# A chunked scan: the state contribution of a row on four column quarters, and placed last in TensorE's turn

## The reference

```
dA_cs  = cumsum(dt * A)                                       # within a chunk
att    = (C B^T) * exp(dA_cs_i - dA_cs_j) * dt_j, causal      # 128 x 128 per head
y      = att @ x  +  exp(dA_cs) * (C @ state)  +  D * x
state  = state * exp(dA_cs[last])  +  B^T @ (exp(dA_cs[last] - dA_cs) * dt * x)
out    = (layernorm(y) * norm_w + norm_b) * z @ out_proj_w^T
```

## Time and profile before

| | us |
|---|---|
| median of 3 runs | 2703.73 |
| lowest and highest | 2697.77, 2711.97 |
| the profiled execution, its own time | 2695.24 |
| its span, first to last instruction | 2693.3 |
| busy PE, PEld, DVE, ACT, POOL | 2309.8, 1650.3, 1685.5, 1305.3, 1184.2 |

### The profile page before, as it was taken

How to read it: one execution, slowest core, us unless ns; L and a number is a source line. 1 busy time by engine, 2 the same in 40 slices (tenths; PEclk the granted TensorE clock), 3 DMA queues, 4 the chain that set the end, 5 groups by cost and what they waited for, 6 DMA issues and landing times. The chain is left out here.

```text
span 2693.3 us, 61840 instructions
## 1 busy us (share of the span) xinstructions
PE 2309.8 (86%) x21973; PEld 1650.3 (61%) x22100; DVE 1685.5 (63%) x3119; ACT 1305.3 (48%) x2719; POOL 1184.2 (44%) x1381
## 2 busy tenths in 40 slices
PE   0798888998758189999999999999987988879888
PEld 0565536796657057777777777777766655356553
DVE  5345475675535278777777777777773454734547
ACT  0345440281057156666666666666643454334543
POOL 0332250000000168788888888888853222532225
PEclk9999998999979589999999999999998999989999
DMA  8613495415523222222222222222215034950349
GB/s 197 188 52 71 109 312 143 90 50 165 131 75 120 102 51 52 53 54 51 51 53 54 51 51 53 54 51 51 54 50 168 20 72 111 310 176 26 70 107 315
DMA packets 287144, 270.22 MB, mean 100 GB/s; under 512 B 157102, under 2 KB 220366, under 8 KB 280730
## 3 DMA queue, kind: packets, MB, share of 16 engines
q1 hardware_dynamic: 276218, 254.04, 33.6%
q0 software_dynamic: 9280, 6.44, 2.0%
q10 hardware_dynamic: 1496, 7.63, 0.8%
HBM read 163.34 MB, written 81.46 MB: 91 GB/s over the span
## 5 line engine op out<-in xcount | busy, mean ns | idle before, releaser
L1608 ACT ACTIVATE l_scan_decay<-l_scan_cum 128x512 f32<-128x512 f32 x384 | 215.5, 595 | 241.5 <-PE l_scan_cum L1505 241.4
L1641 DVE TENSOR_TENSOR l_scan_att<-l_scan_decay,l_scan_causal_scores 128x512 f32<-128x512 f32 x384 | 292.4, 762 | 63.9 <-ACT l_scan_decay L1614 63.7
L709 ACT COPY l_arena<-l_body_bank 128x384 f32<-128x384 f32 x192 | 141.5, 896 | 309.6 <-PE l_body_bank L588 309.6
L1614 ACT ACTIVATE l_scan_decay<-l_scan_decay 128x512 f32<-128x512 f32 x384 | 227.8, 630 | 4.0
L1576 PEld LDWEIGHTS l_scan_gate_projected<-l_scan_yz,l_scan_wo 128*96 128x96 f32 x1536 | 171.0, 163 | 80.3 <-issue 77.5
L803 DVE TENSOR_TENSOR l_freq<-l_body_bank,l_filter 128x512 f32<-128x512 f32 x144 | 99.6, 692 | 183.8 <-PE l_body_bank L601 183.8
L1547 PE MATMUL l_scan_gate_projected<-l_scan_xr,l_wf 97*128 97x128 f32 (+1 forms) x1536 | 205.4, 283 | 1.2 <-DVE l_scan_xo L1695 1.2
L1576 PE MATMUL l_scan_gate_projected<-l_scan_yz,l_scan_wo 128*96 128x128 f32 x1536 | 198.5, 279 | 1.1 <-DVE l_scan_yz L1672 1.1
L568 POOL TENSOR_TENSOR l_arena<-l_arena 96x512 f32<-96x512 f32 x96 | 122.7, 1278 | 170.2 <-ACT l_arena L772 163.3
L1547 PEld LDWEIGHTS l_scan_gate_projected<-l_scan_xr,l_wf 97*128 97x128 f32 (+1 forms) x1536 | 181.0, 190 | 17.7 <-issue 2.7
L642 PE MATMUL l_body_bank<-l_arena 100*64 100x128 f32 x2304 | 148.3, 292 | 50.1 <-DMA l_arena<-l_arena 50.1
(11 more groups left out here) (191 smaller groups left out, 5121.5 us busy)
## 6 DMA issues: line engine op xcount, KB each, us to landing
l_scan_xc<-convolved_rows SPq DMA_DIRECT2D x128, 224.0 KB, 2.8
x_after<-l_arena SPq DMA_DIRECT2D x64, 384.0 KB, 4.8
l_arena<-x_after SPq DMA_DIRECT2D x64, 384.0 KB, 5.6
convolved_rows<-l_slots SPq DMA_DIRECT2D x48, 441.0 KB
l_conv_x_main<-x_after SPq DMA_DIRECT2D x64, 256.0 KB, 2.6
l_arena<-x_after SPq DMA_DIRECT2D x16, 1024.0 KB, 8.0
prepare_xt<-x SPq DMA_DIRECT2D x8, 1536.0 KB
l_arena<-x SPq DMA_DIRECT2D x32, 384.0 KB, 5.5
```

What stands on the lines that cost most here:

```text
L709: nc.scalar.copy(tA[:, b, :, j:j + 2].rearrange("p c q -> p q c"), bank[n % 4][:, 0:2 * C].rearrange("p (q c) -> p q c", q=2)).then_inc(t_ ...
L1608: nc.scalar.activation(decay[:, b % 2, 4 * g:4 * g + 4, :], cum[(b + g) % 2][:], ACT.Relu, scale=-1.0)\
L1614: nc.scalar.activation(group, group, ACT.Exp, scale=-1.0).then_inc(exp_done, 1)
L1641: nc.vector.tensor_tensor(att[:, b, 4 * g:4 * g + 4, :], decay[:, b % 2, 4 * g:4 * g + 4, :], causal[:, b % 2:b % 2 + 1, :].broadcast_to([ ...
```

## The change

The state contribution is computed as four matmuls of 96 channels each (`CH` is 96) instead of one of 384. Each has an output of 32 partitions, and quarter g goes to partitions 32g to 32g + 31 of `p_i`, columns 0 to 95. The four stand behind the out-projection at the end of the turn; the next turn begins with the attention products. VectorE makes the new state in four additions of 32 x 96, each reading another 32 partitions of `p_i` and writing the state's 32 partitions from partition 0. They stand behind the third `att` instead of ahead of it. Only the last of the four matmuls and the last of the four additions raise their semaphore. The waits are the same as before.

```
                     if row0:
                         cumulative(row0, 2)
-                    if row2:
-                        r, b, n = row2
-                        pe.wait_ge(scaled, r + 1)
-                        nc.tensor.matmul(p_i[0:N_STATE], xc[:, b, D_INNER:D_INNER + N_STATE], xw[:, b % 2], start=True, stop=True)\
-                            .then_inc(st_done, 1)
                     if row4:
                         r, b, n = row4
                         pe.wait_ge(yz_done, r + 2)
                         ...
                         last.then_inc(o_done, 1)
+                    if row2:
+                        r, b, n = row2
+                        pe.wait_ge(scaled, r + 1)
+                        for g in range(4):
+                            last = nc.tensor.matmul(p_i[g * N_STATE:(g + 1) * N_STATE, 0:CH], xc[:, b, D_INNER:D_INNER + N_STATE],
+                                                    xw[:, b % 2, g * CH:(g + 1) * CH], start=True, stop=True)
+                        last.then_inc(st_done, 1)
...
                     if row0:
                         attention(row0[0], row0[1], 1)
+                        attention(row0[0], row0[1], 2)
                     if row2:
                         r, b, n = row2
                         dve.wait_ge(st_done, r + 2)
                         dve.wait_ge(faded_done, r + 1)
-                        nc.vector.tensor_tensor(state[:], p_i[0:N_STATE], faded[:], ALU.add).then_inc(state_ready, 1)
-                    if row0:
-                        attention(row0[0], row0[1], 2)
+                        for g in range(4):
+                            last = nc.vector.tensor_tensor(state[:, g * CH:(g + 1) * CH], p_i[g * N_STATE:(g + 1) * N_STATE, 0:CH],
+                                                           faded[:, g * CH:(g + 1) * CH], ALU.add)
+                        last.then_inc(state_ready, 1)
```

## The result

| | before | after |
|---|---|---|
| median, us | 2700.75 (4 runs) | 2776.86 (4 runs, 2773.32 to 2780.42) |
| ratio, 95% interval | | 1.028 (1.0259 to 1.0301) |
| profiled execution, its span | 2693.3 | 2778.5 |

The change makes the kernel 76 us slower. The forecast was slower, by 14 us: the side was right, the size was not, and the range ended at 2740.

What follows compares the result with a forecast made beforehand. TensorE's queue, 8.16 us a turn, was taken to bound the kernel; after the change VectorE's chain, 7.06 + 1.13 + 0.08 = 8.27, would. Over 124 turns that adds 14 us to 2703.73, giving 2718, range 2670 to 2740.

Steps and rivals of the forecast that it cites:

- TensorE bounds before, the chain through ScalarE and VectorE is next, 1.1 us behind: In a scan turn, TensorE's queue fills all 8.16 us; the chain from L1531 back to TensorE is 1.1 us shorter.
- TensorE's queue after, 7.69 us: TensorE's own turn after the change: 8.16 less 0.76 for the old matmul plus 0.29 for the four new ones.
- The state at +7.06: On VectorE, the new state's additions start on average 7.06 us behind L1531's start, after the third att.
- a rival, put on the second att: GpSimd's later work slows VectorE's second att: 0.29 us a turn if whole, 2754 us, or 2736 if half; chance 0.12.
- the shift of 0.44 us that I had worked out for L1658: On VectorE, this instruction (L1656 before the change) comes 0.44 us later in the turn, moving GpSimd's work later too.
- Four additions in series, 1.13 us: VectorE's four 32 x 96 state additions do not overlap: 0.26 us each with 0.03 between, 1.13 in all.
- From the last addition to L1531, 0.08: The step from the end of VectorE's last state addition to TensorE's start of L1531, taken as 0.08 us.
- The clock: TensorE's granted clock in the scan: a fall below 1.00 was named as a term not priced.
- The sum: Whole kernel: a turn of 8.27 instead of 8.16 us, times 124 full turns, makes +14 us.
- the forecast chain of 8.27: From one L1531 to the next through VectorE: 7.06 + 1.13 + 0.08 = 8.27 us, longer than TensorE's 7.69.
- the additions overlap: Rival: VectorE's four additions take 0.71 to 0.80 us in all, so the kernel takes 2666 to 2677 us; chance 0.24.
- the quarters do not run side by side: Rival: TensorE's four matmuls cost 0.76 us like the old one, its turn stays 8.16, kernel 2704 us; chance 0.04.

Runs made afterwards that it cites:

- e1: The changed kernel with the old single contribution matmul and old single addition put back, both at their new places; 2674.2 us, 0.991 of the kernel before.
- e6: The changed kernel with GpSimd's three weighted forms of x computed for one head of twelve, the rest left at zero (computation left out); 2726.7 us.
- e4: The changed kernel with one contribution matmul of 384 columns and four additions that all read partitions 0 to 31; 2692.1 us.
- e5: The changed kernel with five more transposes, same data to the same place, in TensorE's wait ahead of L1527; 2744.6 us.
- e2: The kernel before with four matmuls of 96 columns and four additions of 32 x 96, both at the old places; 2698.8 us.
- e7: The changed kernel with two contribution matmuls of 192 columns and two additions of 32 x 192 instead of four each; 2700.1 us.

## Why the prediction failed, step by step

- *TensorE bounds before, the chain through ScalarE and VectorE is next, 1.1 us behind.* Right. TensorE waits for nothing of the chain before, and in the changed kernel the chain bounds.
- *TensorE's queue after, 7.69 us.* The matmuls cost 0.19 and not 0.29, and the 0.14 of e1 at the out-projection was not in the sum. It did not matter, since the queue is not the bound.
- *The state at +7.06.* This is the step of the sum that failed: it took the first att at the length it had before, 0.93. Without GpSimd beside it, the state starts at +7.03 (e6), so the other parts were good; with it, it is at +7.37. The prediction had this mechanism as a rival, put on the second att, with a chance of 0.12 and 0.29 us as its full price. In the trace it sits mostly on the first att (mean 1.15 us instead of 0.92), little on the second (0.75 instead of 0.69, so the sign that was named for this rival, a mean over 0.75, hardly shows), and it costs 0.34. In the kernel before, the slow first att was nearly free, because the gated y waits for the gate's projection anyway (it starts at +4.03 before, at +3.93 in e6); at 1.26 us the att outlasts that, and the gated y starts at +4.31. GpSimd's side of it: its xw takes 1.3 us in the 94 of 128 rows in which an att lies beside it for 0.58 us or more, and 0.8 in the others. The Trainium skill has the rule, in "SBUF — State Buffer", section "Who interferes with whom": a VectorE instruction with two inputs in SBUF, as att is, contends with a GpSimd instruction that reads SBUF, and the page calls the contention an exclusive lock. e6 agrees (att 0.69 to 0.72 on average beside the narrow forms, up to 1.27 beside the full ones in the changed kernel). I did not carry it through: the shift of 0.44 us that I had worked out for L1658 (it measured 0.42) decides which GpSimd instruction the first att meets.
- *Four additions in series, 1.13 us.* Right; 1.04 measured, and e4 shows the reason, a change of partitions between consecutive instructions, now for an input in PSUM too.
- *From the last addition to L1531, 0.08.* 0.05.
- *The clock.* This is the second failure, a term put at nothing. It was named at the end as not priced, because no turn of the loop before showed a wait on TensorE. By the trace it was worth 29 us: 24 in the ten long turns of the loop over 8.46 each, and 5 in three of the first seven turns of the scan. By e5 it was 32. (Long turns at the start of the scan, 9.55 to 11.56 us, are also in e1, e2 and e7, so not all of the 5 need be the change's.) A forecast of a new wait on TensorE in every turn needed this term.
- *The sum.* 0.11 x 124 = 14 was forecast. Measured: 0.30 x 127 = 38 in ordinary turns and 29 by the clock, 67 of the 67.6 us. Against the forecast chain of 8.27, the state came 0.31 later, the additions were 0.09 shorter and the last step 0.03, which makes 8.46. So that the side was right is luck: with the additions and the last step as measured, the chain that was forecast takes 7.06 + 1.04 + 0.05 = 8.15, no more than before, and the kernel became slower by the two things that the sum left out. Or, against the kernel before and by e6: 43 us (0.34 x 127) are GpSimd's, and all the rest is -5. Some 8 of the 76 us between the medians are open; the profiled executions differ by more than that ahead of the scan. With the clock kept up, e5 took 2744.6, 5 over the 2740 at which the range ended; so the clock makes most of the distance to the range.
- *The rivals.* That the additions overlap is excluded by the trace and e4; that the quarters do not run side by side, by 0.19 us for eight records.

Of the gain that the change was to bring, 0.57 us a turn on TensorE, everything was there and turned into a wait at L1531.

## What to carry to other kernels

Before an instruction is moved later in its engine's turn, add up the ring that leads from it back to the bounding engine, every instruction on it, at the length it has beside its new neighbours. Work saved on the bounding engine is lost as soon as another ring is longer, and here the wait then cost more than its own length, because the clock of TensorE fell. And ask first for the piece of the change that costs the other engines nothing: the move alone gave 26 us, two halves with the state first 54, and the swap on VectorE on top of that 61 in all.

## What the hardware showed that I had not expected

- A 32-column matmul runs beside others on the other column quarters without being split: the first of six records starts 0.01 us behind it (e1).
- Consecutive VectorE additions of 32 x 96 take 0.165 us from start to start when they read the same 32 partitions of PSUM, and 0.26 when each reads another 32 (e4, after).
- When att (128 x 512, both inputs in SBUF) and GpSimd's products of 128 x 384 meet, either can be slowed: att 0.69 or 1.26 us, GpSimd's 0.83 or 1.28 (after).
- With TensorE's weight loads waiting 0.95 us in each turn of 8.46, and its matmuls 0.76, the granted clock fell to its lower level in ten turns out of 110, for up to 6.8 us at a time; with five useless transposes put into that wait, 0.26 us of the matmuls' was left and it did not fall in the loop (e5).
